# Key/value work six steps later, weights requested where they are needed, in a graph and mixer layer on one core

## The reference

```python
xn = _layernorm(x, axis=-1)
x = x + gnn(xn, edge_attr, src, dst, W_gnn, h_bias) + mix(xn[None], ...)[0]
x = x + ffn(_layernorm(x, axis=-1)[None], ...)[0]

def gnn(src_feats, edge_feats, src_idx, dst_idx, weights, h_bias):
    m = src_feats[src_idx] @ weights[:d] + edge_feats @ weights[d:]
    deg = segment_sum(ones, dst_idx)
    norm = where(deg > 0, rsqrt(maximum(deg, 1)), 0)
    return segment_sum(m * norm[dst_idx][:, None], dst_idx) + h_bias

def mix(x, w_qkv, b_qkv, kln_g, kln_b, vln_g, vln_b, w1, b1, w2, b2):
    q, k, v = split((x @ w_qkv + b_qkv) by heads)       # 8 heads of 32
    k, v = _ln(k, kln_g, kln_b), _ln(v, vln_g, vln_b)
    kv = einsum('bhnd,bhne->bhde', k, v) / HW            # a sum over all nodes
    ret = einsum('bhnd,bhde->bhne', q, kv) + x
    return gelu(ret @ w1 + b1) @ w2 + b2 + x

def ffn(x, Wr, br, W1, b1, W2, b2, gamma, beta):
    # routing weights from the mean over all nodes, the top 2 of 8 experts for all of them,
    # two layers with gelu, their weighted sum, a layer norm of result + x
```

## Time and profile before

| | us |
|---|---|
| median of three runs | 1627.36 |
| the profiled execution | 1632.06 |
| its span | 1630.3 |
| TensorE busy | 1173.3 |
| GpSimd busy | 915.7 |
| VectorE busy | 654.6 |
| ScalarE busy | 559.7 |

### The profile page before, as it was taken

The page is one execution under the profiler, slowest core; times in us unless marked ns, Lnnn a source line. Parts: engine busy times, 40 slices in busy tenths (PEclk is TensorE's granted clock), DMA queues, the critical chain, the costliest instruction groups (busy, mean ns, idle before and its releaser), DMA issues.

```text
span 1630.3 us, 22836 instructions
## 1 busy us (share of the span) xinstructions
PE 1173.3 (72%) x7416; PEld 803.1 (49%) x7416; DVE 654.6 (40%) x1698; ACT 559.7 (34%) x1157; POOL 915.7 (56%) x975
## 2 busy tenths in 40 slices
PE   0157767776686777766676767677776839999997
PEld 0033333433343343334445444453554539999997
DVE  5633223323223333221233244243432446676775
ACT  4731111111111111111333343333342457677674
POOL 6166666666666666666666666666666103344342
PEclk9988987888788888778798897889898959999999
DMA  9976666656665666486677787777777341222221
GB/s 234 319 216 202 181 194 185 205 177 180 201 193 174 189 199 181 127 260 204 206 225 232 220 240 248 225 223 241 234 225 238 103 136 40 71 61 76 64 68 39
DMA packets 209235, 295.03 MB, mean 181 GB/s; under 512 B 20940, under 2 KB 180146, under 8 KB 207887
## 3 DMA queue, kind: packets, MB, share of 16 engines
q1 hardware_dynamic: 152899, 165.66, 34.7%
q0 software_dynamic: 39888, 108.97, 22.1%
q10 hardware_dynamic: 16350, 19.20, 3.5%
HBM read 261.75 MB, written 32.00 MB: 180 GB/s over the span
## 4 chain that ended last, share of the span: by engine, by line
another core or an unknown queue 31%; PE 30%; issue 14%; DVE 9%; ACT 9%; DVEq 2%; DMA 2%; SPq 2%; ACTq 1%; POOL 0%; POOLq 0%
PE bank L1156 8%; PE bank L1167 8%; PE bank L944 2%; PE bank L997 2%; PE bank L938 2%; DVEq L1324 2%; PE bank L930 2%; PE bank L1003 1%; ACT fl L649 1%; PE bank L1041 1%; ACT L751 1%; ACT L731 1%; DVE acc L1326 1%; DVE xc L1339 1%
## 5 line engine op out<-in xcount | busy, mean ns | idle before, releaser
L583 POOL DMA_INDIRECT ring<-xn_table,src_sb x807 | 781.8, 969 | 465.7 <-issue 221.1
L930 PE MATMUL bank<-ring,s 128*32 128x512 f32 x1662 | 283.6, 667 | 65.3 <-DVE s L1298 42.6
L944 PE MATMUL bank<-fl_t,wg 128*128 128x128 f32 x1120 | 158.7, 300 | 51.6 <-ACT fl_t L649 36.7
L944 PEld LDWEIGHTS bank<-fl_t,wg 128*128 128x128 f32 x1120 | 146.7, 211 | 54.8 <-ACT fl_t L649 38.8
L938 PE MATMUL bank<-ident,fl 128*128 128x128 f32 x280 | 60.9, 356 | 146.9 <-ACT fl L649 131.7
L1326 DVE TENSOR_TENSOR acc<-acc,bank 128x96 f32 x277 | 70.7, 255 | 226.5 <-issue 87.4
L938 PEld LDWEIGHTS bank<-ident,fl 128*128 128x128 f32 x280 | 39.3, 177 | 222.2 <-ACT fl L649 170.7
L1331 DVE TENSOR_TENSOR xt_lo<-bank,xt_hi 128x250 fp32r<-128x250 f32 (+1 forms) x75 | 37.9, 505 | 260.7 <-ACT xt_hi L649 173.0
L649 ACT ACTIVATE xt_hi<-bank 128x250 fp32r<-128x250 f32 (+1 forms) x75 | 33.4, 446 | 285.6 <-remote 227.3
L712 ACT ACTIVATE kvn<-xc 125x512 f32<-125x512 f32 x50 | 31.5, 630 | 262.1 <-DVE xc L1339 135.3
L1156 PE MATMUL bank<-xf_hi,fw_hi 128*128 128x256 f32 x400 | 113.5, 284 | 9.4 <-DVE fw_lo L1628 7.2
(11 more groups left out here) (221 smaller groups left out, 2374.1 us busy)
## 6 DMA issues: line engine op xcount, KB each, us to landing
ring<-edges SPq DMA_DIRECT2D x207, 512.0 KB
ring<-xn_table,src_sb POOLq DMA_INDIRECT x807
xnr<-xn_table SPq DMA_DIRECT2D x50, 125.0 KB
xnr<-xn_table SPq DMA_DIRECT2D x25, 250.0 KB
xch<-x SPq DMA_DIRECT2D x25, 250.0 KB
base_rows<-xch ACTq DMA_DIRECT2D x25, 250.0 KB
x_rows<-xch ACTq DMA_DIRECT2D x25, 250.0 KB
xt_cols<-xte ACTq DMA_DIRECT2D x25, 250.0 KB
```

Of the source, the lines that this page charges most:

```text
L583: pool.indirect_dma_start(out=to, out_offset=None, in_=rows, in_offset=bass.IndirectOffsetOnAxis(ap=index, axis=0),).then_inc(done, 16)
L930: mm = pe.matmul(ps_seg[t % 2][j * W:(j + 1) * W, :], lhsT=s32[:, t % 3, j * TS + i, :].bitcast(F32), rhs=ring[:, u, j, :], start=i == 0, ...
L944: mm = pe.matmul(ps_y[:, o * P:(o + 1) * P], lhsT=wg[:, c, o * P:(o + 1) * P], rhs=fl_t[:, c, :], start=c == 0, stop=c == 3)
```

## The change

KV0 goes from 2 to 8, so the key/value work of every tile and the folding come six steps later, FOLD goes from 106 to 112, and the lists that are worked out from it move: the first mix goes from step 114 to 120, the last three from 195, 198 and 201 to 201, 204 and 207; the last four node chunks from groups 66, 67, 69 and 71 to 68, 69, 70 and 71. The number of steps stays 225.

SyncE requests `wg` ahead of the edge rows of step 3, the key weights behind those of step 6 and the others behind those of step 8; they stood ahead of the loop. The preparation of the key weights moves into step 7 of the loop, on VectorE and ScalarE; the sum of two biases moves into step 14. VectorE makes the one-hot of group 0 ahead of the row statistics, and it waits for the clearing of `acc` not before the loop but before the first sums. ScalarE takes both roots of the row statistics before it scales the rows.

```diff
-KV0 = 2
+KV0 = 8
@@ sync
             for q in range(RAW):
+                if q == 3:
+                    sp.wait_ge(s_rel, 1)
+                    sp.dma_start(wg[:, :, :], wgnn.rearrange("(c p) d -> p c d", p=P)).then_inc(s_wg, 16)
                 edge_load(q)
-            sp.wait_ge(s_rel, 1)
-            sp.dma_start(wstage[:, :, :], wkv_l.rearrange("(c p) d -> p c d", p=P)).then_inc(s_wkv, 16)
...
             sp.wait_ge(s_tab, TABLE_DONE)
+
+            def key_weights():
+                sp.dma_start(wstage[:, :, :], wkv_l.rearrange("(c p) d -> p c d", p=P)).then_inc(s_wkv, 16)
+                sp.dma_start(bkv[:, :], bkv_l.partition_broadcast(TN)).then_inc(s_wkv, 16)
+                for j, row in enumerate((kln_g, vln_g, kln_b, vln_b)):
+                    sp.dma_start(lns[:, j, :], row.partition_broadcast(P)).then_inc(s_par, 16)
+
+            def mix_weights():
+                sp.dma_start(wq_sb[:, :, :], wq_t.rearrange("(c p) d -> p c d", p=P)).then_inc(s_par, 16)
...
             for q in range(TS * STEPS):
                 if RAW <= q < NQ:
                     edge_load(q)
+                if q == RAW:
+                    key_weights()
+                if q == RAW + 2:
+                    mix_weights()
@@ scalar
                 nc.scalar.activation(sdg[:, tiles], veg[:, tiles], ACT.Sqrt).then_inc(s_gsd, 1)
+            for h in range(2):
+                tiles = slice(h * RAW * ST // 2, (h + 1) * RAW * ST // 2)
                 act.wait_ge(s_gr, h + 1)
...
-            act.wait_ge(s_wprep, 2)
-            copy(wkv_hi[:, :, :], wstage[:, :, :]).then_inc(s_wsplit, 1)
...
+                if q == KV0 - 1:
+                    act.wait_ge(s_wprep, 2)
+                    copy(wkv_hi[:, :, :], wstage[:, :, :]).then_inc(s_wsplit, 1)
                 if i == 1 and 1 <= t <= NG:
                     evict_t(t - 1)
@@ tensor
                     if t == 1:
-                        pe.wait_ge(s_par, 16 * 11)
+                        pe.wait_ge(s_wg, 16)
                     project(t - 1)
@@ vector
-            raw_stats(0)
-            raw_stats(1)
-            raw_scales(0)
-            raw_scales(1)
...
-            one_hot(0)
-
-            v.wait_ge(s_wkv, 16 * 2)
...
-            v.wait_ge(s_zero, 1 + NB)
+            def row_bias():
+
+                v.wait_ge(s_par, 16 * 10)
+                v.tensor_tensor(brows[:, :], brows[:, :], hrows[:, :], ALU.add).then_inc(s_br, 1)
+                v.wait_ge(s_br, 1)
+
+            def key_weights():
+
+                v.wait_ge(s_wkv, 16 * 2)
+                wv = wstage[:, :, :].rearrange("p c (g e) -> p (c g) e", e=HC)
+                v.tensor_reduce(wmean[:, :], wv, AX, ALU.add).then_inc(s_wprep, 1)
...
+            one_hot(0)
+            raw_stats(0)
+            raw_stats(1)
+            raw_scales(0)
+            raw_scales(1)
...
                 if i == 2 and 1 <= t <= NG:
+                    if t == 1:
+                        v.wait_ge(s_zero, 1 + NB)
                     sums(t - 1)
+                if q == KV0 - 1:
+                    key_weights()
+                if q == KV0 + 6:
+                    row_bias()
```

More of the change, by code:

```diff
@@ L253, in gps_layer @@
         s_w2, s_rw, s_fb = s_wkv, s_src, s_par
-        W2, ROUTER, FFN_ROWS = 16 * 2 + 16, 16 + 32, 16 * 11 + 16 * 6
+        W2, ROUTER, FFN_ROWS = 16 * 2 + 16, 16 + 32, 16 * 10 + 16 * 6
         s_load = [sem(f"s_load{b}") for b in range(NB)]
@@ L259, in gps_layer @@
         s_gst, s_gmv, s_gve, s_gsd, s_grc, s_gr, s_raw = (sem(f"s_{n}") for n in ("gst", "gmv", "gve", "gsd", "grc", "gr", "raw"))
-        s_id, s_const, s_iota, s_mask, s_d, s_dp, s_rel, s_wprep, s_wsplit = (sem(f"s_{n}") for n in (
-            "id", "const", "iota", "mask", "d", "dp", "rel", "wprep", "wsplit"))
+        s_id, s_const, s_iota, s_mask, s_d, s_dp, s_rel, s_wprep, s_wsplit, s_wg = (sem(f"s_{n}") for n in (
+            "id", "const", "iota", "mask", "d", "dp", "rel", "wprep", "wsplit", "wg"))
         s_e, s_gat = ([sem(f"s_{n}{u}") for u in range(RS)] for n in ("e", "gat"))
@@ L458, in _ @@
[L458 to L463, removed]
@@ new lines, in mix_weights @@
+            def mix_weights():
+                sp.dma_start(wq_sb[:, :, :], wq_t.rearrange("(c p) d -> p c d", p=P)).then_inc(s_par, 16)
+                sp.dma_start(bq[:, :], bq_l).then_inc(s_par, 16)
+                sp.dma_start(w1_sb[:, :, :], w1.rearrange("(c p) d -> p c d", p=P)).then_inc(s_par, 16)
+                sp.dma_start(b1c[:, :], b1_l).then_inc(s_par, 16)
+                sp.dma_start(brows[:, :], b2.partition_broadcast(TN)).then_inc(s_par, 16)
+                sp.dma_start(hrows[:, :], hbias.partition_broadcast(TN)).then_inc(s_par, 16)
+                sp.dma_start(wr_sb[:, :, :], wr.rearrange("(c p) e -> p c e", p=P)).then_inc(s_rw, 16)
+                sp.dma_start(rt[0:1, 0, :], br.partition_broadcast(1)).then_inc(s_rw, 16)
@@ L958, in fold_weights @@
                 if step == 0:
+                    pe.wait_ge(s_par, 16 * 10)
                     pe.wait_ge(s_cs, 4)
@@ L1299, in one_hot @@
                                 wide(rel[:, c:c + m], m, W), ALU.is_equal).then_inc(s_hot, 1)
-            one_hot(0)
-            v.wait_ge(s_wkv, 16 * 2)
-            wv = wstage[:, :, :].rearrange("p c (g e) -> p (c g) e", e=HC)
-            v.tensor_reduce(wmean[:, :], wv, AX, ALU.add).then_inc(s_wprep, 1)
-            v.wait_ge(s_wprep, 1)
-            v.scalar_tensor_tensor(wv, wide(wmean[:, :], KC * GR, HC), -1.0 / HC, wv, ALU.mult, ALU.add).then_inc(s_wprep, 1)
-            bv = bkv[:, :].rearrange("p (g e) -> p g e", e=HC)
-            v.tensor_reduce(lnst[:, 0, :], bv, AX, ALU.add).then_inc(s_wprep, 1)
-            v.wait_ge(s_wprep, 3)
-            v.scalar_tensor_tensor(bv, wide(lnst[:, 0, :], GR, HC), -1.0 / HC, bv, ALU.mult, ALU.add).then_inc(s_wprep, 1)
-            v.wait_ge(s_par, 16 * 11)
-            v.tensor_tensor(brows[:, :], brows[:, :], hrows[:, :], ALU.add).then_inc(s_br, 1)
-            v.wait_ge(s_wsplit, 1)
-            v.tensor_tensor(wkv_lo[:, :, :], wstage[:, :, :], wkv_hi[:, :, :].bitcast(F32), ALU.subtract).then_inc(s_wsplit, 1)
-            v.wait_ge(s_wprep, 4)
-            v.wait_ge(s_br, 1)
-            v.wait_ge(s_zero, 1 + NB)
+            def row_bias():
[6 more added lines that the diff above has]
+                v.tensor_reduce(wmean[:, :], wv, AX, ALU.add).then_inc(s_wprep, 1)
+                v.wait_ge(s_wprep, 1)
+                v.scalar_tensor_tensor(wv, wide(wmean[:, :], KC * GR, HC), -1.0 / HC, wv, ALU.mult, ALU.add).then_inc(s_wprep, 1)
+                bv = bkv[:, :].rearrange("p (g e) -> p g e", e=HC)
+                v.tensor_reduce(lnst[:, 0, :], bv, AX, ALU.add).then_inc(s_wprep, 1)
+                v.wait_ge(s_wprep, 3)
+                v.scalar_tensor_tensor(bv, wide(lnst[:, 0, :], GR, HC), -1.0 / HC, bv, ALU.mult, ALU.add).then_inc(s_wprep, 1)
+                v.wait_ge(s_wsplit, 1)
+                v.tensor_tensor(wkv_lo[:, :, :], wstage[:, :, :], wkv_hi[:, :, :].bitcast(F32), ALU.subtract).then_inc(s_wsplit, 1)
+                v.wait_ge(s_wprep, 4)
             def sums(t):
```

6 lines of the change are left out of this document (removed).

## The result

The changed kernel takes 1631.39 us (median of 20 runs, 1625.5 to 1643.5) against 1627.48 us for the kernel before (20 runs beside it): ratio 1.0026, interval 1.0013 to 1.0038. A second comparison (run e5_changed) gave 1632.49 against 1627.48 us, 1.0025 (1.0011 to 1.0039). The forecast was 1630 us. The change makes the kernel slower by 4 us, a little under what one short measurement tells from no change.

What follows compares the result with a forecast made beforehand. Bound: GpSimd's 5.0 us a step plus about 1 us wait in the edge phase, then TensorE and a chain between engines. Terms -7.5 - 0.8 + 10.8 = +2.5 us on the median 1627.36 gave 1630 us, range 1624 to 1637.

Steps and rivals of the forecast that it cites:

- the start: Start of the edge phase, up to gather 11: earlier by 7.5 us, bounds 0 and -13.
- The first step: Step 0 after the prefetched rows' statistics: scaling starts sooner, so gather 6 goes out 5.5 us earlier.
- nothing if the rows haven't landed: Lower bound on the 5.5 us won at step 0: no gain if rows and table haven't landed.
- The second hold: Gathers 10 and 11, behind ScalarE's clearing and copy of group 0: 5.9 and 7.7 us earlier.
- Steps without key/value work: Steps 2 to 8: 0.13 us saved a step, 0.8 us in all; what is won stays won.
- The rival with a lead of 13 us: Start: unnamed waits don't come, gather 17 is 13 us early; -5.8 us in all, 1621.6 us, chance 0.24.
- The lower clock: Steps 3 to 8: TensorE with less to do pays 0.9 us a step; sum the same or 1 us worse.
- Requests, preparation, bias at nothing: Start: moved weight requests, key preparation in step 7 and bias sum at step 14 cost nothing; uncovered, 7 or 5 us.
- The end: From step 202 to the reduction of the means: later mixes and node chunks cost +10.8 us, bounds +5 and +17.
- the part ahead of the last strips: Steps 202 to 209: three products and two turns, less one turning of node rows, +5.8 us.
- From there on nothing is changed: After the reduction of the means at 1314.65 us: the rest of the kernel stays as it was.
- The sign I named: If right, strips of step 202 to the reduction of the means take some 50.6 us instead of 39.8.

Runs made afterwards that it cites:

- e5_changed: The changed kernel measured once more against the kernel before, on a slow chip: 1632.49 against 1627.48 us.
- e8: Changed kernel with key/value work at step 5, clearing on VectorE and row scales in halves: 1624.95 against 1627.48 us of the kernel before.
- e3: Kernel before with only the first one-hot ahead of the row statistics and both roots before the scaling; fast chip, 1477.27 against 1477.56 us.
- e6: Changed kernel with the accumulator cleared by VectorE instead of ScalarE: 1630.92 against 1627.48 us of the kernel before.
- e4: Kernel before with only key/value work begun at step 8 and packed tables of mixes and node chunks; fast chip, 1487.44 against 1477.56 us.
- e1: Changed kernel with the end of the kernel before (first mixes packed, last mix at 201); fast chip, 1479.83 against 1477.56 us.
- e12_late: Kernel before with only the changed kernel's later mixes and node chunks; slow chip, 1635.81 against 1627.33 us.
- e10: Changed kernel with the end of the kernel before (first mixes packed, last mix at 201); slow chip, 1625.89 against 1627.33 us.
- e11: Changed kernel with key/value work at step 5 and mixes packed, last at 201: 1621.60 against 1627.33 us of the kernel before.
- e7: Changed kernel with key/value work at step 5 instead of 8, last mix at 204: 1623.29 against 1627.48 us of the kernel before.

## Why the prediction was right

It said -7.5 for the start, -0.8 for lighter steps, +10.8 for the end: +2.5 us. The profiles say -9.6 up to gather 204, +10.5 to the mean, +1.6 behind it, +0.5 for S: +3.0; the medians say +3.9 and +5.0. By its own steps:

- *The first step*, -5.5: -4.9 from S, of which the one-hot gives 0.5 back, so -4.4. ScalarE scaled at S + 10.3 us, TensorE followed 2.2 us later, as worked out. But the forecast had gather 6 go out 1.8 us behind the first strips; it does so 2.7 us behind them in both kernels, and did in its own rows (70.13 and 72.87 us). The bound "nothing if the rows haven't landed" was close: the rows had little slack to spare (e8), and on the fast chip none (e3).
- *The second hold*, -5.9 and -7.7 us: -5.8 and -7.4 (gathers 10 and 11). The wait ahead of gather 10 is the clearing on ScalarE (e6), though gather 10 gains only 1 us without it.
- *Steps without key/value work*, -0.8: wrong in sign. Between gathers 11 and 17 1.1 us of the lead is lost, and by e4 lighter steps alone bring nothing on the fast chip. That a lead is then kept holds: -6.3 at gather 17, -7.0 at gather 114. The rival with a lead of 13 us is out. The lower clock that the prediction named for these steps is there (0.76 for 0.81 in steps 6 to 17); whether it is part of the 1.1 us isn't shown.
- *Requests, preparation, bias at nothing*: no cost appears in the sum, but the argument missed that on the fast chip the start's lead comes only with them (e4 and e3 against e1). On the slow chips, whose times the forecast is about, no run has the new order without the moved requests.
- *The end*, +10.8 up to the mean: 71.6 us for 61.1, +10.5. The sum is right, its two terms are not. Counted from gather 204, the part ahead of the last strips grew by 2.2 us (forecast +5.8, in part because some of the mix work falls out ahead of gather 204, see below), the part behind them by 8.2 us (forecast +5.0). Behind the last strips TensorE has 24 more matmuls and 6.9 us more busy time (6.6 in the second profiles), where the forecast priced 18 at 2.5 us; the granted clock there is 0.64 instead of 0.73, and the forecast counted the products at the higher level. The TensorE page of the Trainium skill ("TensorE: Matmul & The Clock Gate", Part 1: The HAM clock gate) has an idle TensorE drop to the lower clock. These rows don't show that as the cause of the lower share here: behind the last strips TensorE is idle for 9.6 of 17.2 us before and for 11.0 of 25.5 us in the changed kernel, so its busy share went up.
- *"From there on nothing is changed"*: wrong by 1.6 us. From the mean to the end it takes 317.4 and 317.1 us before, 318.8 and 319.1 in the changed kernel, 319.3 in e12_late, 317.1 and 317.9 in e10 and e11, 318.8 and 317.1 in e7 and e8. It is there in every kernel with mixes two groups late; by what, I did not find.
- *Left out of the sum*: moving mixes behind gather 204 takes them out of the steps ahead of it. That gives back 2.6 us in the changed kernel and 4.0 in e12_late. It offset the 1.6 us behind the mean and the 0.5 us of S, which is luck.
- *The sign I named*, 50.6 us from the strips of step 202 to the mean, came out at 57.0 us (1260.81 to 1317.84 us). It was a bad marker: in the kernel before those strips stand 21 us behind gather 204, in the changed one 15 us (17 in its second profile, 54.2 us by this sign). Counted from the gather the same end fits.

```profile
1260.81 1.06 PE L943 MATMUL bank<-ring,s 128*32 128x512 f32 x8
...
1317.84 0.20 DVE L1548 TENSOR_REDUCE mean_c<-mean_p 128x2 f32<-128x50 f32 x1 [5.43 <-ACT xte L786]
```

So the account was right as a whole: a lead of about 7 us is made at the start and kept, and a longer end of 10.5 us spends it. The number was right partly by luck, because errors of both signs cancelled, within the end and between it and the rest.

## What to carry to other kernels

Work begun later for the sake of the start must end later or be packed: look for the smallest delay that makes room for what really gains (here 3 steps gave the whole lead of 6 at gather 17, and a third of the price at the end), and before packing look at the margin between a tile's store and the engine that writes over it. Count a lead from the last event that both kernels share, and take two profiles before believing a difference of a few us. Removing one hold at a start is worth only what the next one behind it leaves, here 1 us of 11.

## What the hardware showed unexpectedly

One program, one input: 1627.5, 1627.3 and 1477.6 us on three chips. A gather costs the same on each (0.95 us and 0.30 us to the next); what differs is GpSimd's waits between them. Its waits in the edge phase, kernel before on a slow chip, are the earlier trace rows, 245 us, the 37.5 us before gather 6 among them. On the fast chip the waits that lead nowhere are gone; GpSimd's in e3_first, whose time is that of before:

```profile
POOL ring L583 <- issue: 240.1, 787, 0.5
...
POOL ring L583 <- PE bank L932: 59.4, 20, 32.6
```

and the pace up to step 114 is 5.1 us a step instead of 5.9. On the slow chips one wait of up to 3 us a group comes for a semaphore whose sender, by the records, was done long before. ScalarE and VectorE have such waits too (the 9.47 us above). Why is open: the trace names no releaser. It matters for a change like this one: on the fast chip TensorE waits for edge rows in the steps with mixes (up to 9.9 us at a time), on the slow ones at most 4.2 us at a time in the profiles of before, the changed kernel and e10_pack. The lead of e1_pack over e3_first is 11.7 us at gather 17, 8.5 at gather 114 and 10.9 at gather 159; at gather 177 e1 is 2.6 us behind, and at gather 204 1.3 ahead. The lead goes where e1's waits for stored base rows stand, and e4_kvonly loses 7.2 us on e3 in the same steps. What the transfers would have taken without them, these runs don't tell.
